# Expert weights split in three pieces, placed by a table; four-tile loops on ScalarE and VectorE; x in four slots

## The chip, the core and the metric

The kernel runs on one core of a Trainium2 chip. Its engines are TensorE (matmuls; PE in the profile, with PEld for the loads of its stationary operand), VectorE (DVE), ScalarE (ACT), GpSimd (POOL) and SyncE (SP), and 16 DMA engines that SP, ACT and POOL hand transfers to. Each engine works through its own list of instructions in order, and they meet at semaphores alone. An engine's sequencer also does what the profile does not count as busy: register arithmetic, branches, loads of registers from memory, waits, and handing out DMAs. The metric is the device time of one execution in microseconds (us).

## The reference

Cut to what matters (B = 8 batches of 256 rows of 512; 2048 tokens for the second part; E = 32 experts, 8 for each token, inner width I = 192):

```python
x = x + xattn(layernorm(x), ctx)          # attention over 8 batches; not touched by the change
xt = layernorm(x).reshape(-1, 512)        # 2048 tokens
probs = softmax(xt @ gate_w.T)            # 32 experts
full_w = top-8 of probs, scaled to sum 1, zero elsewhere
g = silu(einsum('th,ehi->eti', xt, w_gate))
u = einsum('th,ehi->eti', xt, w_up)
y = einsum('eti,eih->eth', g * u, w_down)
out = x + einsum('eth,te->th', y, full_w)
```

## The kernel before

**Two stages.** The first runs over the 8 batches (attention, layer norm, router). GpSimd scatters each normalised row, with its 32 expert weights and its token number behind it (512 + 33 floats), into the DRAM tensor `x_sorted`, once for each of its 8 experts and ordered by expert. The second stage is the expert layer. It runs over tiles of 128 sorted rows: 144 tiles in this data, 4 to 6 for each of the experts. Small tables, made on VectorE at the end of the first stage, say for each tile where its rows begin (`x_row`), which expert it belongs to, and what is to be done beside it.

**Precision.** Each matmul operand is a float32 split in two: a high part rounded to float32r (`_hi`, written by ScalarE with a copy) and the rest (`_lo`, by a subtraction on VectorE). Each product is then three matmuls (hi*hi, hi*lo, lo*hi). This holds for the tile's rows (`xT_hi`, `xT_lo`), for the activations (`aA_hi`, `aA_lo`, `aB`) and for the weights of each expert: `w_raw` (loaded), `w_hi` and `w_lo`, each in two halves for experts of even and odd number, with 1536 columns of gate and up and 1024 of down.

**One tile j**, as `ffn` of each engine has it:

- SP, `load_tile`: one register load of the row number (L365); four DMAs of the 128 x 512 floats (L373) and one of the 33 floats behind each row (L375), into slot j % 8. It first waits until VectorE's product of tile j - 8 is done (`act_ready`).
- PE: the gate and up product of tile j (12 matmuls, L1228, L1229, L1232); the transposes of tile j - 1's activation (L1188, L1189); the down product of tile j - 2 (5 matmuls, L1205 to L1209). Ahead of the last, its sequencer waits for the `_lo` part of that activation and for the bank (L1199). Ahead of the first it loads two registers, the count of experts that are needed and the half of the weights (L1214).
- ACT: silu of tile j (L632), `xT_hi` of tile j + 2 (L611), the high part of the activation of j - 1 (L616, L617), evacuation of y of j - 2 (L624). Then, where the table says so, the load of coming raw weights (`load_coming_raw`, two DMAs, L301 and L303), the copy of an expert's down weights (L520) and of its gate and up weights (L525). L630 is its register load, of two values.
- DVE: the transposition of tile j + 2 in blocks of 32 (L961); a register load of three values (L979); where the table says so the subtraction for an expert's down weights (L745) and gate and up weights (L751); a copy of the token numbers out of the slot (L992); silu * up * weight (L995); `xT_lo` of j + 2 (L965); the low parts of the activation of j - 1 (L972, L973).
- POOL: an indirect DMA that adds y of tile j to the rows of `out` that the token numbers name (L465). At an expert's first tile it waits until all earlier adds have landed.

**Where the weights are split.** At the first tile of expert e the tables name expert e + 1. ACT copies its gate and up columns at the end of that tile's step and its down columns in the next, and issues the raw load of expert e + 3 in the step after. DVE follows one step behind each: one piece of 1536 columns and, a step later, one of 1024.

**What sets the order.** All is written by hand. `run_tiles` unrolls 8 tiles, and then loops over eights with two conditional bodies of 4 tiles, as many as the data needs (36 fours here, out of at most 40); all five engines use it.

## Time and profile before

| | us |
|---|---|
| median of 3 runs | 860.26 |
| lowest and highest | 858.43, 863.49 |
| the profiled execution, as timed | 863.78 |
| its span, first to last instruction | 862.1 |
| PE busy in the span | 731.4 |
| DVE, ACT, POOL busy | 578.6, 436.5, 369.0 |

The span is 1.7 us shorter than the time of the same execution. The first stage takes about the first 265 us, and the tiles run from there to the end, at a granted TensorE clock of 1.00 of full speed for nearly all of it. In the lists, a start is in us from the start of the span; a second number is a duration; an entry in brackets is the idle time of that engine ahead of the instruction, and what ended it. "issue" means that nothing which the profile shows was waited for, which leaves the engine's own sequencer. A line name that ends in q (SPq, DVEq, ACTq, PEldq) is work of such a sequencer.

### The profile page before, as it was taken

The page shows a single profiled execution, that of the slowest core. Times are in us where ns is not written, and L with a number is a line of the kernel's source. Part 1 is how long each engine was busy: PE and PEld are TensorE (multiplying, and loading weights), DVE is VectorE, ACT ScalarE, POOL GpSimd, SP SyncE. Part 2 cuts the span into 40 slices and gives each one's busy share as a digit, 9 for nine tenths or more (in the row PEclk, how much of TensorE's full clock was granted, in tenths as well). Part 3 has the DMA queues.
Part 4 walks back from the last instruction along what each step waited for, and adds up shares of the span by engine and source line. Part 5 has one row for each costly group of instructions (what it writes and reads, how often), then busy time and mean ns, then how long its engine had stood idle before and what let it go on. Part 6 is the DMA issues. An engine that isn't in the chain of part 4 may idle for free.

```text
span 862.1 us, 21273 instructions
## 1 busy us (share of the span) xinstructions
PE 731.4 (85%) x3655; PEld 590.7 (69%) x3656; DVE 578.6 (67%) x1464; ACT 436.5 (51%) x1021; POOL 369.0 (43%) x294
## 2 busy tenths in 40 slices
PE   7998788795554389999999999999999989989994
PEld 5554444454344378888788788888878878878883
DVE  5584665575434266777877767877787777777773
ACT  2771544254110155566655565656655665655652
POOL 1015644765447233434344443434434443443443
PEclk9998999996776699999999999999999999999998
DMA  9976644554466479999999999999999999999975
GB/s 303 369 229 253 228 160 175 228 177 181 168 227 214 144 129 211 247 217 212 208 243 200 209 224 202 197 202 251 206 212 236 226 193 227 231 205 199 198 123 73
DMA packets 174394, 179.73 MB, mean 208 GB/s; under 512 B 36864, under 2 KB 128768, under 8 KB 174368
## 3 DMA queue, kind: packets, MB, share of 16 engines
q0 software_dynamic: 30976, 73.48, 39.2%
q1 hardware_dynamic: 119248, 68.09, 30.7%
q10 hardware_dynamic: 24144, 37.89, 14.0%
q8 instruction: 8, 0.13, 0.1%
q14 instruction: 18, 0.15, 0.0%
HBM read 92.25 MB, written 87.13 MB: 208 GB/s over the span
## 4 chain that ended last, share of the span: by engine, by line
PE 62%; issue 12%; DVE 7%; another core or an unknown queue 5%; SPq 4%; ACT 3%; DVEq 2%; DMA 2%; ACTq 1%; POOL 1%; POOLq 0%
PE bank L1228 12%; PE bank L1229 10%; PE bank L1232 10%; PE bank L1205 4%; PE bank L1206 3%; PE bank L1207 3%; PE bank L1209 3%; PE bank L1208 3%; SPq L373 2%; PE bank L1060 2%; PE bank L1188 2%; PE bank L1189 2%; PE bank L1126 1%; PE bank L1132 1%
## 5 line engine op out<-in xcount | busy, mean ns | idle before, releaser
L465 POOL DMA_INDIRECT out_dram<-ctx_all,tile_token x144 | 233.2, 1619 | 336.7 <-ACT ctx_all L624 182.2
L1228 PE MATMUL bank<-w_hi,xT_hi 128*128 x576 | 202.5, 351 | 39.6 <-issue 26.3
L1229 PE MATMUL bank<-w_lo,xT_hi 128*128 x576 | 196.6, 341 | 0.0
L420 POOL DMA_INDIRECT x_sorted<-xn_kept,slots x112 | 116.8, 1043 | 135.8 <-issue 87.1
L1228 PEld LDWEIGHTS bank<-w_hi,xT_hi 128*128 128x128 f32 x576 | 109.6, 190 | 69.4 <-issue 66.1
L632 ACT ACTIVATE probT<-bank 128x192 f32<-128x192 f32 x144 | 47.1, 327 | 164.2 <-PE bank L1232 127.1
L1232 PE MATMUL bank<-w_hi,xT_lo 128*128 x576 | 124.5, 337 | 0.0
L961 DVE STREAM_TRANSPOSE x_all<-x_all 128x512 f32<-128x512 f32 x146 | 103.9, 711 | 30.0 <-DMA x_all<-x_sorted 20.4
L611 ACT ACTIVATE xT_hi<-x_all 128x512 fp32r<-128x512 f32 x146 | 91.5, 627 | 62.9 <-DVE x_all L961 61.6
L1229 PEld LDWEIGHTS bank<-w_lo,xT_hi 128*128 128x128 f32 x576 | 109.9, 191 | 2.8
L1232 PEld LDWEIGHTS bank<-w_hi,xT_lo 128*128 128x128 f32 x576 | 103.1, 190 | 0.0
L965 DVE TENSOR_TENSOR xT_lo<-x_all,xT_hi 128x512 fp32r<-128x512 f32 x146 | 100.6, 689 | 1.7 <-issue 0.7
L995 DVE SCALAR_TENSOR_TENSOR probT<-probT,x_all,bank 128x192 f32<-128x192 f32 x144 | 59.0, 410 | 56.8 <-ACT probT L632 51.7
L624 ACT ACTIVATE ctx_all<-bank 128x512 f32<-128x512 f32 x144 | 85.7, 595 | 19.3 <-PE bank L1209 14.5
L751 DVE TENSOR_TENSOR w_lo<-w_raw,w_hi (+1 forms) x32 | 56.2, 1758 | 40.1 <-issue 39.0
L1205 PE MATMUL bank<-w_hi,aA_hi 128*128 x144 | 69.1, 480 | 15.1 <-issue 8.8
L1206 PE MATMUL bank<-w_lo,aA_hi 128*128 x144 | 56.8, 395 | 0.0
L1207 PE MATMUL bank<-w_lo,aB 128*128 x144 | 56.6, 393 | 0.0
L1209 PE MATMUL bank<-w_hi,aB 128*128 x144 | 56.3, 391 | 0.0
L1208 PE MATMUL bank<-w_hi,aA_lo 128*128 x144 | 56.2, 390 | 0.0
L525 ACT ACTIVATE w_hi<-w_raw (+1 forms) x32 | 47.6, 1488 | 12.5 <-issue 7.0
L1188 PE MATMUL bank<-ident,probT 128*128 128x128 f32 x144 | 39.4, 274 | 4.1 <-DVE probT L995 2.9
(198 smaller groups left out, 1123.2 us busy)
## 6 DMA issues: line engine op xcount, KB each, us to landing
x_all<-x_sorted SPq DMA_DIRECT2D x584, 64.0 KB
w_raw<-in_w_gate_up_dram ACTq DMA_DIRECT2D x28, 768.0 KB
w_raw<-in_w_down_dram ACTq DMA_DIRECT2D x28, 512.0 KB
x_sorted<-pad_rows SPq DMA_DIRECT2D x1, 8720.0 KB, 31.3
x_all<-in_x_dram SPq DMA_DIRECT2D x8, 512.0 KB
ctx_all<-in_ctx_dram SPq DMA_DIRECT2D x8, 512.0 KB
out_dram<-x_all SPq DMA_DIRECT2D x8, 512.0 KB
w_raw<-in_w_gate_up_dram SPq DMA_DIRECT2D x4, 768.0 KB
```

The lines of the kernel that those rows point to most:

```text
L420: pool.indirect_dma_start(out=x_sorted, out_offset=bass.IndirectOffsetOnAxis(ap=to[:, u, k:k + 1], axis=0), in_=rows[:, u, :], in_offset=N ...
L465: pool.indirect_dma_start(out=out, out_offset=bass.IndirectOffsetOnAxis(ap=tile_token[:, k:k + 1], axis=0), in_=y_sb[:, i, :], in_offset=N ...
L611: act_e.activation(xT_hi[:, s, :], xb[:, s, :], ACT.Copy).then_inc(S["xT_hi_ready"], 1)
L624: act_e.activation(y_sb[:, i, :], bank[6 + i % 2][:], ACT.Copy).then_inc(S["y_evac"], 1)
L961: dve.transpose(xb[:, i % 2, :].rearrange("p (c b t) -> p b c t", c=HC, b=HC), xg[:, i, :]).then_inc(S["xT_ready"], 1)
L965: dve.tensor_tensor(xT_lo[:, s, :], xb[:, s, :], xT_hi[:, s, :].bitcast(F32), ALU.subtract).then_inc(S["xT_lo_ready"], 1)
L1205: pe.matmul(out_y, aA_hi[:, s, :], part(w_hi, GU_END, DA_END), start=True, stop=False)
L1206: pe.matmul(out_y, aA_hi[:, s, :], part(w_lo, GU_END, DA_END), start=False, stop=False)
L1207: pe.matmul(out_y, aB[:, s, :], part(w_lo, DA_END, WCOLS), start=False, stop=False)
L1228: pe.matmul(out_gu, xT_hi[:, s, c * P:(c + 1) * P], gate_up(w_hi, c), start=(c == 0), stop=False)
L1229: pe.matmul(out_gu, xT_hi[:, s, c * P:(c + 1) * P], gate_up(w_lo, c), start=False, stop=False)
L1232: m = pe.matmul(out_gu, xT_lo[:, s, c * P:(c + 1) * P], gate_up(w_hi, c), start=False, stop=(c == HC - 1))
```

## The change

It touches the second stage and the tables ahead of it.

- **Pieces.** `w_raw`, `w_hi` and `w_lo` become six buffers: `gu_raw`, `gu_hi`, `gu_lo` with four pieces of 768 columns (gate and up of two experts in two pieces each), and `down_raw`, `down_hi`, `down_lo` with two of 1024.
- **Table.** For each tile one number tells VectorE how many gate and up pieces and how many down pieces are to be done by then, and the expert. Within an expert, the due count rises by one gate and up piece at its second tile, by another at its third, and by one down piece at its fourth, all of the next expert. With four tiles or more for each expert there is one piece a tile, in three tiles one after another. ScalarE's number is that of the tile after, and has a bit for the expert's first tile. Each engine keeps counts of what it has done in registers, and compares.
- **Register loads.** One value a tile on DVE (was three), ACT (two) and PE (two); the parts are taken out of the number with shifts and masks. PE works out half and count from one number.
- **Raw load.** ACT issues it at the first tile of an expert, for the expert after the next.
- **Token numbers.** The copy L992 and its wait are gone; POOL's add takes them from the slot itself.
- **x.** The 512 floats of a tile go to one of four slots, and SP waits for the transposition of tile j - 4. The 33 floats behind them keep eight slots, are issued two tiles later than the rows, and wait until the add of tile j - 8 has landed, and for the load of j - 4. So SP has two more waits a tile, each of which raises a counter (`wait_apart`).
- **Loops.** ACT and DVE unroll 8 tiles and then loop over fours (`run_quarters`); PE, SP and POOL stay with eights.

```diff
-        xg = x_all[:, 0:SLOTS, :]
+        xg = x_all[:, 0:4, :]
...
+        def run_quarters(eng, step):
+            turns = load_turns(eng)
+            for k in range(SLOTS):
+                step(k // 4, k % 4)
+            with eng.Fori(2, NT // 4) as q:
+                with eng.If(q < turns):
+                    for k in range(4):
+                        step(q, k)
...
+            def load_x(eight, k):
+                i = k % 4
+                sp.reg_load(row_reg[i], x_row[0:1, bass.ds(SLOTS * eight + k, 1)])
...
-                    sp.wait_ge(S["act_ready"], SLOTS * (eight + n - 1) + i + 1)
+                if not is_before(eight, k, 4):
+                    sp.wait_ge(S["xT_ready"], SLOTS * eight + k - 3)
...
-                sp.dma_start(xw[:, i, :], rows[:, H:RW]).then_inc(xg_loaded[i], 16)
+            def load_w(eight, k):
+                if not is_before(eight, k, SLOTS):
+                    wait_apart(sp, "sp_passed", (added[k % 4], 16 * (quarter(eight, k) - 1)))
+                if not is_before(eight, k, 4):
+                    wait_apart(sp, "sp_passed", (xw_loaded[k % 4], 16 * quarter(eight, k)))
+                sp.dma_start(xw[:, k, :], rows_at(k)[:, H:RW]).then_inc(xw_loaded[k % 4], 16)
...
-                    for k in range(2, 6):
-                        load_tile(eight, k)
+                    for k in range(4):
+                        load_w(eight, k)
+                        load_x(eight, k + W_BEHIND)
...
             def ffn(q, k):     # ACT, after evac_y
+                split_gu_hi(read_bits(act_e, gu_due_reg, due_reg, 7, 0, 2 * E))
+                split_down_hi(read_bits(act_e, down_due_reg, due_reg, 1, 63, E))
+                load_coming_raw(read_bits(act_e, first_reg, due_reg, 0, 1, 1))
...
+            def load_coming_raw(is_first):
+                with act_e.If(is_first > 0):
+                    e = act_e.snap(coming_reg, min_val=4, max_val=E - 1)
+                    wait_apart(act_e, "act_passed", (S["gu_ready"], 2 * e - 2), (S["down_ready"], e - 1), (S["raw_loaded"], 32 * e))
+                    load_raw(act_e, e, act_e.snap(e & 1, min_val=0, max_val=1))
...
+            def split_gu_lo(gu_due, level=0):     # DVE; ACT's split_gu_hi has the same form
+                done = dve.snap(gu_done_reg, min_val=4, max_val=2 * E)
+                with dve.If(done < gu_due):
+                    wait_apart(dve, "dve_passed", (S["gu_hi_ready"], done + 1))
+                    piece = dve.snap(done & 3, min_val=0, max_val=3)
+                    dve.tensor_tensor(gu_lo[:, bass.ds(piece, 1), :], gu_raw[:, bass.ds(piece, 1), :],
+                                      gu_hi[:, bass.ds(piece, 1), :].bitcast(F32), ALU.subtract).then_inc(S["gu_ready"], 1)
+                    dve.reg_alu(gu_done_reg, gu_done_reg, 1, ALU.add)
+                    if not level:
+                        split_gu_lo(gu_due, 1)
...
-                pe.reg_load([found_reg, half_reg[i]], tile_needs[0:1, bass.ds(j, 1), :].rearrange("p a b -> p (a b)"))
+                pe.reg_load(found_reg, experts_in[0:1, bass.ds(j, 1)])
                 pe.reg_alu(experts_reg[i], found_reg, 1, ALU.max)
+                pe.reg_alu(half_reg[i], experts_reg[i], 1, ALU.add)
+                pe.reg_alu(half_reg[i], half_reg[i], 1, ALU.bitwise_and)
+                pe.reg_alu(gu_need_reg, experts_reg[i], 2, ALU.mult)
```

```order
L979 TENSOR_LOAD dve_needs
L980 ISA
L984 COMPARE_AND_BRANCH
L236 REGISTER_ALU
L745 ISA [waits down_hi]
L745 TENSOR_TENSOR w_lo<-w_raw,w_hi 128x1024
L984 UNCONDITIONAL_BRANCH
L293 ISA
L987 COMPARE_AND_BRANCH
L236 REGISTER_ALU
L751 ISA [waits gate_up_hi]
L751 TENSOR_TENSOR w_lo<-w_raw,w_hi 128x1536
```

And after:

```order
L1045 TENSOR_LOAD dve_due
L308 REGISTER_ALU
L310 REGISTER_ALU
L311 ISA
L1017 COMPARE_AND_BRANCH
L237 REGISTER_ALU
L1020 REGISTER_ALU [waits gu_hi_ready]
L1020 ISA
L1020 TENSOR_TENSOR gu_lo<-gu_raw,gu_hi 128x768
L1022 ISA
L1017 COMPARE_AND_BRANCH
L237 REGISTER_ALU
```

The one subtraction of 1536 columns stood last, behind the place of the down piece; now a piece of 768 stands first, a second comparison stands nested behind it, and the down piece (still 1024 columns) follows after that.

**The order on SP** in the tile loop, from the small DMA of the 33 floats to the first large one of the next rows; before:

```order
L375 ISA
L375 DMA x_all<-x_sorted 128x33
L365 ISA
L365 TENSOR_LOAD x_row
L366 ISA
L373 ISA [waits act_ready]
L373 DMA x_all<-x_sorted 32x4x128
```

And after:

```order
L378 ISA [waits added1,xw_loaded1]
L399 DMA x_all<-x_sorted 128x33
L383 ISA
L383 TENSOR_LOAD x_row
L378 ISA [waits xT_ready]
L390 DMA x_all<-x_sorted 32x4x128
```

The small DMA, which waited for nothing, has two waits ahead of it and belongs to the tile two before the rows that follow; the rows wait for the transposition where they waited for the product.

## Rows read from the trace of the kernel before

**Rows 1.** Two stretches: busy PE, PEld, DVE, ACT, POOL; clock, DMA share, GB/s.

```profile
318.00:453.00 135.00, 126.77 (x656) 110.88 (x655) 101.50 (x226) 78.24 (x188) 55.23 (x35) 0.99 1.00 220
500.00:800.00 300.00, 281.50 (x1476) 246.88 (x1475) 228.28 (x500) 178.72 (x422) 124.86 (x77) 1.00 0.99 214
```

**Rows 2.** PE: first transpose of two tiles; then its count, first and last start.

```profile
496.92 0.27 PE L1188 MATMUL bank<-ident,probT 128*128 128x128 f32 x1
...
500.39 0.27 PE L1188 MATMUL bank<-ident,probT 128*128 128x128 f32 x1
...
L1188 PE MATMUL bank<-ident,probT x78: 272/272/272, 500.4 to 798.5; 128*128 128x128 f32 x78
```

**Rows 3.** Groups of instructions, 300 to 800 us: count, busy us, mean ns.

```profile
L751 DVE TENSOR_TENSOR w_lo<-w_raw,w_hi x28 | 49.2, 1758 | 36.9 <-issue 35.8 <-ACT w_hi L525 1.1
...
L525 ACT ACTIVATE w_hi<-w_raw x28 | 41.7, 1489 | 11.7 <-issue 6.6 <-DMA w_raw<-in_w_down_dram 5.0
...
L745 DVE TENSOR_TENSOR w_lo<-w_raw,w_hi x28 | 33.1, 1183 | 0.0
...
L992 DVE COPY tile_token<-x_all 128x1 int32<-128x1 int32 x129 | 18.5, 144 | 24.5 <-issue 21.8 <-DMA out_dram<-ctx_all,tile_token 1.8
```

**Rows 4.** DVE in order of time, ahead of one gate and up subtraction.

```profile
494.94 0.71 DVE L961 STREAM_TRANSPOSE x_all<-x_all 128x512 f32<-128x512 f32 x1
497.05 1.76 DVE L751 TENSOR_TENSOR w_lo<-w_raw,w_hi  x1 [1.40 <-issue]
```

**Rows 5.** ACT in order of time, around one load of raw weights.

```profile
503.05 0.43 ACTq L301 DMA_DIRECT2D w_raw<-in_w_gate_up_dram  x1
...
505.31 0.33 ACT L632 ACTIVATE probT<-bank 128x192 f32<-128x192 f32 x1 [2.60 <-PE bank L1232]
```

**Rows 6.** Register loads: ns min/median/max, first and last start.

```profile
L979 DVEq TENSOR_LOAD <-dve_needs x144: 741/1076/1679, 294.6 to 844.7; - x144
...
L1214 PEldq TENSOR_LOAD <-tile_needs x144: 532/540/1479, 265.7 to 842.5; - x144
...
L365 SPq TENSOR_LOAD <-x_row x146: 4/276/1049, 264.2 to 826.7; - x146
```

**Rows 7.** SP's small DMA in 318:453 and 500:800: count, first and last.

```profile
L375 SPq DMA_DIRECT2D x_all<-x_sorted x38: 68/364/569, 320.0 to 451.8; - x38
...
L375 SPq DMA_DIRECT2D x_all<-x_sorted x78: 14/364/737, 501.4 to 799.7; - x78
```

**Rows 8.** SP's waits in these two stretches: total us, times, longest.

```profile
SPq L373 <- DVE probT L995: 1.7, 1, 1.7
...
SPq L373 <- DVE probT L995: 32.3, 31, 2.4
```

**Rows 9.** SP in order of time: tiles 2, 7, 10, 11 and 145.

```profile
290.69 1.86 SPq L373 DMA_DIRECT2D x_all<-x_sorted  x4
...
305.47 3.59 SPq L373 DMA_DIRECT2D x_all<-x_sorted  x4
...
318.06 1.78 SPq L373 DMA_DIRECT2D x_all<-x_sorted  x4
...
321.06 1.86 SPq L373 DMA_DIRECT2D x_all<-x_sorted  x4
...
827.91 1.88 SPq L373 DMA_DIRECT2D x_all<-x_sorted  x4
```

**Rows 10.** DVE in order of time: transposition of tiles 2, 7 and 145.

```profile
294.60 0.71 DVE L961 STREAM_TRANSPOSE x_all<-x_all 128x512 f32<-128x512 f32 x1 [2.32 <-DMA x_all<-x_sorted]
...
312.81 0.71 DVE L961 STREAM_TRANSPOSE x_all<-x_all 128x512 f32<-128x512 f32 x1 [2.37 <-DMA x_all<-x_sorted]
...
845.29 0.71 DVE L961 STREAM_TRANSPOSE x_all<-x_all 128x512 f32<-128x512 f32 x1
```

**Rows 11.** POOL in order of time: two adds, the second of a first tile.

```profile
500.09 1.55 POOL L465 DMA_INDIRECT out_dram<-ctx_all,tile_token  x1 [2.90 <-ACT ctx_all L624]
506.16 1.55 POOL L465 DMA_INDIRECT out_dram<-ctx_all,tile_token  x1 [4.51 <-issue]
```

306 lines of the change are left out of this document (157 added, 149 removed).

## The prediction

> **What bounds the kernel now.** I read first how long a tile takes, then who is late when it takes longer, then who could not go faster. The first stage is not touched; the tiles fill the span from about 265 us on. In 500 to 800 us PE is busy 281.5 of 300 us and DVE 228.3 [rows 1], but PE's busy time is modelled, so I take the distance between equal instructions. An undisturbed tile takes 500.39 - 496.92 = 3.47 us; 78 of them start between 500.4 and 798.5, so the mean is 298.1 / 77 = 3.87 us [rows 2]. So 0.40 us a tile is lost. There are 28 subtractions of each kind for 129 tiles [rows 3], one for 4.6 tiles, which makes the loss 1.8 us for each expert.
>
> Where it comes from: the long piece. After the transposition at 494.94 (ended 495.65) DVE stands idle for 1.40 us for its own sequencer and then subtracts for 1.76 us [rows 4]; the product for that tile (L995) and the low parts that PE's down product waits for are behind it on DVE. The 1.40 us are mostly the register load of three values, 0.74 to 1.68 us, behind the dispatch of the transposition, and two branches [rows 6]. PE then pays twice, as its own load of two values (0.54, at most 1.48 us) stands behind its wait ahead of the down product, and has to be done before the next tile's first matmul [rows 6]. ACT has one more: the sequencer hands out the raw weights from 503.05 on, 0.43 us for the first of two DMAs, and the next silu starts at 505.31 [rows 5].
>
> Who could not go much faster: **SP**. In 318 to 453 us it issues 38 small DMAs from 320.0 to 451.8, (451.8 - 320.0) / 37 = 3.56 us a tile [rows 7], and waits for only 1.7 us in all of it [rows 8]. So 3.52 us a tile is SP's own pace. In 500 to 800 us it needs (799.7 - 501.4) / 77 = 3.87 us, of which 32.3 us are waits: own pace (298.3 - 32.3) / 77 = 3.45. An undisturbed tile takes SP 321.06 - 318.06 = 3.00 us [rows 9]; the rest are hand-outs that stick, as the 3.59 us for four that otherwise take 1.86 [rows 9]. SP's own 3.48 us (mean of the two) is PE's 3.47. Today SP is ahead only because PE loses 0.40 us a tile.
>
> **The change, part by part.**
>
> *Pieces.* A piece of 768 columns is half of L751's and L525's 1536: 1758 / 2 = 0.88 us on DVE, 1489 / 2 = 0.75 on ACT [rows 3], both perhaps 0.03 more for the fixed part. The work stays the same in sum, but one tile now gets 0.88, 0.88 and 1.18 us in three tiles, instead of 1.76 and 1.18 in two. DVE's busy time a tile is 228.3 / 77.5 = 2.95 us with its share of the subtractions, (1.76 + 1.18) / 4.6 = 0.64 [rows 1, 3], so 2.31 without them and 2.17 without the copy of 0.14 (L992). With 0.88 that is 3.05, with 1.18 it is 3.35: both fit into 3.47 if the engine doesn't wait for its sequencer, while 2.31 + 1.76 = 4.07 did not. This takes the largest part of the 1.8 us an expert from PE.
>
> *Register loads.* One value takes SP 0.28 us, two take PE 0.54, three take DVE 0.74 at least and 1.08 in the median [rows 6]: some 0.25 us a value. I take 0.3 to 0.5 us off on DVE, 0.25 on ACT and PE; against it DVE gets some eight register steps and one comparison more, ACT about the same, PE three. At 0.08 us a step (below) that gives 0.3 to 0.6 us back, in the sequencer, beside the engine's work except ahead of a piece. I count nothing for the sum of both (bounds: 0.3 us a tile either way on the chain silu, product, low parts). The Trainium skill ("DMA: Bandwidth & Descriptors", latency and other measured facts) gives a register load from memory a floor of about 600 ns, whatever its size; by that rule one value would save DVE 0.14 us at least time and PE nothing, and SP's median of 0.28 us speaks against it.
>
> *Raw load.* It stays on ACT, at 1.1 us of its sequencer for each expert, now in the tile that also has a piece of 0.75 us where it had none. That keeps part of the loss: 0.3 to 1.0 us an expert, 0.07 to 0.22 a tile. It is issued one expert (at least 4 tiles, 13.9 us) ahead of its use. 1.31 MB take 6.1 us at the whole 214 GB/s of that stretch and 12.2 at half of it [rows 1], so it arrives in time.
>
> *x in four slots.* The rows can be fetched four tiles ahead, 13.9 us. From SP's first hand-out to the transposition it took 294.60 - 290.69 = 3.9 us at tile 2 and 312.81 - 305.47 = 7.3 us at tile 7, where DVE waited for the data both times [rows 9, 10]. Both fit into 13.9; cost nothing, unless SP itself is late.
>
> *Two more waits on SP.* They are the one thing that the change adds to the engine with no reserve. The order shows the same steps else. SP's 3.00 us are 1.86 for four DMAs, 0.36 for the small one, 0.28 for the register load, and 0.50 for some six register steps [rows 6, 7, 9]: 0.08 each. Two waits that raise a counter, each with its register step at times, then cost 0.16 to 0.26 us; I take 0.18. What is queued behind them are the rows of tile j + 2, and DVE waits for those. Whether the waits themselves hold: the add of tile j - 8 has to land; an add lands within 506.16 - 500.09 = 6.1 us of its issue even when the next one waits for it [rows 11], and SP is a lot later than that.
>
> *Rest.* The tables need about as many small steps as before, while SP is fetching the first tile. Two more empty rounds of the loop on ACT at the end: 0.4 us by my estimate.
>
> **The sum.** SP's new pace is 3.48 + 0.18 = 3.66 us. Nothing ahead of tile 10 is faster for SP, whose rows it hands out at 318.06 [rows 9]. 135 tiles later it reaches tile 145: 318.1 + 135 x 3.66 = 812.2 us, where it was at 827.9 with a lead that it now doesn't have. From hand-out to transposition 5 us (bounds 3.9 and 7.3), to the end as before 862.1 - 845.3 = 16.8 us [rows 10], and 0.4: 812.2 + 5 + 16.8 + 0.4 = 834.4 us of span. That is 27.7 less than 862.1. The profiled execution took 863.78 us, so it would be 836.1; the median of the runs is 860.26, so it would be **832.6**. PE's own sum agrees: floor 3.47 and 0.07 to 0.22 for the raw load are 3.54 to 3.69 us a tile.
>
> **The rivals.**
>
> *PE sets the pace* (821). SP's sticking hand-outs become rarer, as its fetches no longer run 17 us ahead (827.91 to 845.29 today [rows 9, 10]), or its waits cost next to nothing. Then a tile takes 3.47 us and some 0.1 for what is left on ACT, 3.58. Tiles 7 to 145 took 845.29 - 312.81 = 532.5 us [rows 10], 3.86 each; 138 x 3.58 = 494 is 38.5 less: 822. With nothing left at all it is 138 x 3.47 = 479, 807. For it: 32.3 us of waits show that SP has gone at PE's pace. Against it: in 318 to 453 us SP never waits and is no faster than 3.52.
>
> *Half a gain* (846). The pieces still start late: after a transposition come a load, six register steps, a branch, and only then 0.88 us. If DVE loses 0.5 us at each of three pieces, and ACT the raw load's 1.0, 2.5 us of 4.6 x 3.47 = 16.0 hardly fit, and with the SP waits added in the same tiles 3.75 to 3.77 us a tile remain: 138 x 0.1 = 13.8 less, 846.
>
> *The DMA engines set the pace* (no change, 857 to 861). Their busy share is 0.99 at 3.87 us a tile [rows 1]. If that were a wall, no tile could be shorter, and SP's sticking hand-outs would be its sign. The Trainium skill (its first page, "Trainium Kernel Development and Optimization", key constraints) says that the queues of SP, ACT and POOL run on the same 16 engines and interleave; by this rule three queues add up and the share is a sum over queues. Against it as a wall: the share is 1.00 in the first stretch too [rows 1], where SP fetched a tile in 3.56 us for 135 us.
>
> *Slower than before: the ring of eight and four slots.* A tile's add has to land before the 33 floats of the tile eight later are fetched, and the rows of the tile ten later stand behind that on SP. Around this ring: evacuation to add at most 4.5 us (an expert's first tile), landing 6.1 [rows 11], SP 0.5, fetch 7.3 [rows 9, 10], and about 4.5 tiles from transposition to evacuation, 15.6 at 3.47. That is 34.0 us for ten tiles, 3.4 a tile, each at its worst. It decides from 34.7 us on and makes the kernel slower from 10 x 3.87 = 38.7, that is if waits and landings together take 4.7 us longer than the worst read here, at every tile. At 7 us longer it is 4.10 us a tile: 138 x 0.24 = 33 more, 893.
>
> **How the numbers follow.** SP's pace 0.42; PE's pace 0.21; half a gain 0.18; DMA wall 0.12; the ring 0.07. The prediction is that of the first, 832.6, and its own range 822 (own pace 3.45 and 0.13 more) to 845 (3.52 and 0.26, fetch 7.3). The range of 8 in 10 takes in the second from 813 on, and the third; it ends where the wall begins, at 856. What a measurement can tell from no change is about 0.5%, 4.3 us. Faster by more than that: 0.42 + 0.21 + 0.18 and a sliver of the wall's case, 0.82. Within it: 0.10. Slower: 0.08.
>
> **What the profile after would show.** Right: SP's small DMA once in 3.6 to 3.7 us with almost no waits; DVE waits for x at many transpositions, as at tiles 2 and 7; two pieces of about 0.9 and one of 1.2 us in three tiles; PE's undisturbed tile still 3.47. Wrong: SP waits for `xT_ready` in long sums (then PE or DVE sets the pace); SP's wait for the adds shows up (the ring); DMA share 0.99 at an unchanged 3.86 (the wall); idle time for "issue" ahead of each piece of over 0.5 us (half a gain); ACT waits for raw weights, which I priced at nothing.

## The result, and the profile after

Four executions of the changed kernel beside four of the kernel before on the same chip: median 900.85 us (894.5 to 911.39) against 861.88 (858.43 to 875.75), a ratio of 1.044 with a 95% interval of 1.033 to 1.056. The ratio is of the fast executions alone: 911.39 and 875.75, each over 1.5% above the fastest of its kernel, are left out of it. The prediction was 832.6 us and faster; the kernel became slower. The profiled execution took 911.39 us, of which the span is 909.4, the longest of the four; so where sizes matter I use a second trace of the same kernel, from the experiments (829.9 us of span, on another chip; the kernel before has 790.7 on one like it). Both tell the same story.

The tile loop first, as PE's first transposition of each tile: count, duration and the first and last start, of the changed kernel, then of the kernel before on the same chip, then of the kernel before on a chip of the experiments.

```profile
L1248 PE MATMUL bank<-ident,probT x144: 270/272/476, 300.6 to 893.9; 128*128 128x128 f32 x144
```
```profile
L1188 PE MATMUL bank<-ident,probT x144: 272/272/331, 296.5 to 849.1; 128*128 128x128 f32 x144
...
L1188 PE MATMUL bank<-ident,probT x144: 272/272/415, 225.2 to 777.7; 128*128 128x128 f32 x144
```

143 tiles apart, (893.9 - 300.6) / 143 = 4.15 us a tile after, (849.1 - 296.5) / 143 = 3.86 before, and 3.86 again on the other chip. I call this the mean tile from here on; it can be read from one row of any trace. 593.3 - 552.6 = 40.7 us of the 47.3 us by which the span grew are in it. Now the two stretches of [rows 1] again (busy PE, PEld, DVE, ACT, POOL; clock, DMA share, GB/s):

```profile
318.00:453.00 135.00, 120.34 (x619) 102.80 (x618) 92.88 (x186) 75.42 (x183) 50.74 (x33) 1.00 0.90 192
500.00:800.00 300.00, 273.38 (x1357) 236.20 (x1357) 203.31 (x402) 167.80 (x402) 111.28 (x71) 0.95 0.91 198
```

PE fell from 281.5 busy us to 273.4 of 300 and DVE from 228.3 to 203.3; the DMA engines' share, which was 0.99 to 1.00, is 0.90 and 0.91. Nobody is busier. So somebody waits more, and the page says who: two lines of its costliest groups (count, busy us, mean ns, idle before and its releasers), and the chain of the work that ended last.

```profile
L1004 DVE STREAM_TRANSPOSE x_all<-x_all 128x512 f32<-128x512 f32 x146 | 103.9, 712 | 76.3 <-DMA x_all<-x_sorted 70.0
...
L656 ACT ACTIVATE xT_hi<-x_all 128x512 fp32r<-128x512 f32 x146 | 91.6, 628 | 101.2 <-DVE x_all L1004 79.0
...
PE 25%; DMA 23%; issue 16%; SPq 9%; DVE 7%; another core or an unknown queue 7%; ACTq 4%; ACT 3%; DVEq 3%; POOL 2%; POOLq 1%
DMA out_dram<-ctx_all,x_all 12%; DMA x_all<-x_sorted 10%; SPq L390 6%; PE bank L1290 3%; PE bank L1291 3%; PE bank L1294 3%; PE bank L1265 2%; POOL x_sorted L448 1%; PE bank L1143 1%; PE bank L1151 1%; SPq L399 1%; PE bank L1185 1%; PE bank L1269 1%; SPq L383 1%
```

The transposition of x now waits 70.0 us for rows (20.4 before), and ScalarE, which takes its high parts, 79.0 us for the transposition (61.6 before). The chain was 62% PE before; now it is 25% PE and 23% DMA, with the adds at the head of its lines and the rows behind them. That is the pattern of the rival that I had given 0.07. SP's waits for the adds, 500 to 800 us, then its small DMA in the same stretch (answering [rows 7, 8]):

```profile
SPq L238 <- DMA out_dram<-ctx_all,x_all: 40.6, 22, 3.2
...
L399 SPq DMA_DIRECT2D x_all<-x_sorted x70: 7/364/705, 501.8 to 798.1; - x70
```

Where did time go within one turn of the ring? Tiles 51 and 61, all engines in order of time: transposition of tile 51, evacuation of its result, its add, the small DMA of tile 59 (which waited for that add), the rows of tile 61 behind it, and their transposition.

```profile
498.38 0.71 DVE L1004 STREAM_TRANSPOSE x_all<-x_all 128x512 f32<-128x512 f32 x1
...
515.81 0.60 ACT L669 ACTIVATE ctx_all<-bank 128x512 f32<-128x512 f32 x1
...
523.25 1.55 POOL L493 DMA_INDIRECT out_dram<-ctx_all,x_all  x1 [7.40 <-issue]
...
528.82 0.36 SPq L399 DMA_DIRECT2D x_all<-x_sorted  x1
529.78 1.89 SPq L390 DMA_DIRECT2D x_all<-x_sorted  x4
...
540.12 0.71 DVE L1004 STREAM_TRANSPOSE x_all<-x_all 128x512 f32<-128x512 f32 x1 [3.31 <-DMA x_all<-x_sorted]
```

From 498.38 to 540.12 are 41.7 us for ten tiles, where undisturbed ones take 34.7. The add waited 523.25 - 516.41 = 6.8 us on GpSimd, because it is the first of an expert and the ones ahead of it had not landed; it landed and let SP go 5.6 us later; the rows took 540.12 - 529.78 = 10.3 us, for 3.31 of which DVE stood waiting.

One more thing grows out of the waits. In 500 to 800 us the granted TensorE clock is 0.95 of full speed, where it was 1.00. In the traces it is either at full speed or at half (2.4 or 1.2 GHz). In the second trace it is at half for 20.5 us of the tile loop, and in the same loop without the ring (run e1 below) never. Ahead of one such stretch, at 692.5 us, PE was busy only 5.33 of 10 us. At half speed PE does half the work, so up to 10 us of what the ring costs there come by way of the clock, an estimate from these stretches.

### The profile page after: what moved, and what is told of

Read it like the earlier page. It is cut to its first block, busy times and chain, and to the rows that moved or that the text cites. A ratio compares the mean times of both kernels' runs of the same rounds, so it can differ in the third digit from the quotient of the medians.

```text
span 909.4 us, 23919 instructions
## 1 busy us (share of the span) xinstructions
PE 761.1 (84%) x3655; PEld 604.0 (66%) x3656; DVE 567.6 (62%) x1351; ACT 442.0 (49%) x1051; POOL 363.7 (40%) x293
## 4 chain that ended last, share of the span: by engine, by line
PE 25%; DMA 23%; issue 16%; SPq 9%; DVE 7%; another core or an unknown queue 7%; ACTq 4%; ACT 3%; DVEq 3%; POOL 2%; POOLq 1%
DMA out_dram<-ctx_all,x_all 12%; DMA x_all<-x_sorted 10%; SPq L390 6%; PE bank L1290 3%; PE bank L1291 3%; PE bank L1294 3%; PE bank L1265 2%; POOL x_sorted L448 1%; PE bank L1143 1%; PE bank L1151 1%; SPq L399 1%; PE bank L1185 1%; PE bank L1269 1%; SPq L383 1%
## 5 line engine op out<-in xcount | busy, mean ns | idle before, releaser
L493 POOL DMA_INDIRECT out_dram<-ctx_all,x_all x144 | 227.4, 1579 | 385.2 <-ACT ctx_all L669 194.9
L1290 PE MATMUL bank<-gu_hi,xT_hi 128*128 x576 | 206.9, 359 | 21.2 <-issue 18.7
L1291 PE MATMUL bank<-gu_lo,xT_hi 128*128 x576 | 200.3, 348 | 0.0
L1290 PEld LDWEIGHTS bank<-gu_hi,xT_hi 128*128 128x128 f32 x576 | 113.0, 196 | 51.7 <-issue 47.7
L1294 PE MATMUL bank<-gu_hi,xT_lo 128*128 x576 | 125.2, 338 | 0.0
L1291 PEld LDWEIGHTS bank<-gu_lo,xT_hi 128*128 128x128 f32 x576 | 113.2, 197 | 2.9
L1294 PEld LDWEIGHTS bank<-gu_hi,xT_lo 128*128 128x128 f32 x576 | 104.4, 192 | 0.0
L669 ACT ACTIVATE ctx_all<-bank 128x512 f32<-128x512 f32 x144 | 85.6, 594 | 20.4 <-PE bank L1269 17.9
L1265 PE MATMUL bank<-down_hi,aA_hi 128*128 x144 | 70.8, 492 | 28.4 <-DVE aB L1039 17.2
L1248 PE MATMUL bank<-ident,probT 128*128 128x128 f32 x144 | 40.7, 282 | 30.0 <-DVE probT L1052 20.0
L1269 PE MATMUL bank<-down_hi,aB 128*128 x144 | 58.2, 404 | 0.0
L1267 PE MATMUL bank<-down_lo,aB 128*128 x144 | 58.0, 403 | 0.0
```

Of the source, the lines that this page charges most:

```text
L493: pool.indirect_dma_start(out=out, out_offset=bass.IndirectOffsetOnAxis(ap=xw[:, k, E:E + 1].bitcast(I32), axis=0), in_=y_sb[:, i, :], in_ ...
L669: act_e.activation(y_sb[:, i, :], bank[6 + i % 2][:], ACT.Copy).then_inc(S["y_evac"], 1)
L1265: pe.matmul(out_y, aA_hi[:, s, :], part(down_hi, 0, H), start=True, stop=False)
L1269: pe.matmul(out_y, aB[:, s, :], part(down_hi, H, DN), start=False, stop=True).then_inc(S["y_done"], 1)
L1290: pe.matmul(out_gu, xT_hi[:, s, c * P:(c + 1) * P], gate_up(gu_hi, c), start=(c == 0), stop=False)
L1291: pe.matmul(out_gu, xT_hi[:, s, c * P:(c + 1) * P], gate_up(gu_lo, c), start=False, stop=False)
```

## Experiments

The runs e1 to e4, e5 to e8 and e9 to e16 were made on three further chips, on which the kernel before takes nearly the same time: 793.9, 795.0, and 794.1 and 791.5 us in the median. On the last of them it was traced, with a mean tile of 3.86 as on the first. So I compare their times with each other; each ratio is to the kernel before beside it, and differences of medians across chips are good to some 3 us. The changed kernel runs at 829.5 there, its version with a token copy at 796.7. SP's totals of waits for adds below have one part that costs nothing: behind the last fetch SP waits once more for the last adds, 14 to 21 us in three or four waits in the kernels with the ring. Where I give a total "up to the last fetch", that part is taken off. The edits are shown in short form, cut to what matters. The expectations of the first four runs (e1 to e4) were written on the first chip's scale, where the kernel before takes 862; on these chips everything is some 67 us shorter, ahead of the tiles, and their times have to be read that much lower. Expectations speak of theories: 1 the ring; 2 four slots for x are too few; 3 pieces, branches and short loops cost; 4 the ring costs little on these chips; 5 to 9 are explained where they come up.

**e1_token_copy and e5_after_again: is it the ring?**

```diff
-  sp: wait added[k % 4] >= 16 * (quarter(eight, k) - 1)
+  sp: wait act_ready >= SLOTS * (eight - 1) + k + 1
+  dve: wait added[k] >= 16 * (q - 1)
+  dve.tensor_copy(tile_token[:, slot], token column of xw[slot])
-  pool: offsets from xw[:, k, E:E + 1]
+  pool: offsets from tile_token[:, k:k + 1]
```

> The changed kernel, but VectorE copies each tile's token numbers into a buffer of eight, as the kernel before does, and SP's fetch of the 33 floats waits for the product of tile j - 8 (act_ready) instead of its add; x stays in four slots, all else stays. Theory 1 (ring: SP's wait for the add of tile j - 8 holds back the rows of tile j + 2 behind it): the wait is gone, SP runs up to four tiles ahead, the time falls to what I had forecast for SP's own pace, 825 to 850 us. Theory 2 (four slots of x are too few for the fetch): no gain, 885 to 905. Theory 3 (the pieces, the nested branches or the four-tile loops cost the time on VectorE and ScalarE): no gain, 890 to 905.

> The changed kernel itself, unaltered, to stand beside the others on one chip. Theory 1 (ring): a tile takes 4.1 us here as well, and the time is 1.03 to 1.05 of the kernel before; the version with the token copy is below it by 25 to 45 us. Theory 4 (the table's pieces alone bring nothing, and the ring costs little on a chip with quicker transfers): within 1.5% of the kernel before.

Measured: 796.7 us, 1.005 of the kernel before (1.002 to 1.009), against 829.5, 1.043 (1.038 to 1.048) for the changed kernel. SP's and DVE's waits of the changed kernel, then DVE's in the token copy version:

```profile
SPq L238 <- DMA out_dram<-ctx_all,x_all: 97.9, 51, 9.3
...
DVE x_all L1004 <- DMA x_all<-x_sorted: 49.2, 29, 6.5
```

```profile
DVE x_all L1005 <- DMA x_all<-x_sorted: 14.5, 6, 5.2
```

The ring costs 33 us: with it gone DVE's waits for rows fall from 49.2 to 14.5 us. Up to the last fetch SP's waits for adds are 79.8 us of the 97.9, in 47 times. Theory 1 holds for the ring, 2 falls (x still has four slots), 4 falls. But 796.7 is not 832.6 / 860.3 of the kernel before, which would be 769: the pieces' gain of 28 us isn't there either. That was a second error, and the rest of the runs divide between the two. Theory 3, which foresaw no gain from this edit, is not the whole cause; these 28 us are what is left of it.

**e2_ahead_3 and e3_ahead_1: the ring's length.** `W_BEHIND = 2` becomes 3, and 1; the second has one more fetch behind the loop.

> The changed kernel with one number changed: SP issues the rows of tile j + 3, not j + 2, behind the 33 floats of tile j. Theory 1 (ring): the ring is eleven tiles long instead of ten; with the 41 us that it takes on average now, a tile takes 41 / 11 = 3.73 us instead of 4.1, some 50 us less: 845 to 865 us. Theory 2 (four slots): rows still at most four tiles ahead, and SP doesn't wait for slots now: little, 880 to 900. Theory 3 (pieces and loops): unchanged, 895 to 905.

> The changed kernel with the rows of tile j + 1 behind the 33 floats of tile j (and one more fetch behind the loop). Theory 1 (ring): nine tiles, 41 / 9 = 4.55 us a tile, some 60 us more: 945 to 975 us. Theories 2 and 3: slots and pieces are as they were, so at most 10 us more: 895 to 912.

Measured: 802.5 us (1.009, 1.005 to 1.013) and 879.1 (1.106, 1.099 to 1.113). A ring of 9, 10, 11 tiles gives 879, 830, 802: one tile less costs 50 us (60 expected), one more brings 27 (50 expected). The order is the ring's, the proportion isn't quite: a turn isn't of one length, it takes 9 x 4.43 = 39.9, 10 x 4.11 = 41.1 and 11 x 3.94 = 43.3 us by the mean tiles, since with more tiles in the ring it binds less often.

**e6_loading_alone: the other half of the change.** The kernel before with the changed loading and ring, splitting in its two long pieces.

> The kernel before with the loading of the changed kernel alone: x in four slots, the 33 floats fetched apart and eight tiles round, SP waiting for the add of tile j - 8, GpSimd reading the token numbers there, no copy on VectorE. The splitting stays in two long pieces. Theory 1 (ring): this part alone makes it slower, by the whole difference between the changed kernel and the version with the token copy: 1.03 to 1.05 of the kernel before, with SP waits for adds of 50 us and more. Theory 3 (pieces and loops cost the time): same as the kernel before, 0.99 to 1.01.

Measured: 800.9 us, 1.0075 (1.005 to 1.010). SP waits for adds 53.4 us, 35.8 of them up to the last fetch, yet it costs 6 us, not 33:

```profile
SPq L237 <- DMA out_dram<-ctx_all,x_all: 53.4, 25, 9.4
...
DVE x_all L976 <- DMA x_all<-x_sorted: 23.1, 15, 3.8
```

By its number this is theory 3's case, but e1 had spoken against it: there the pieces stayed and 33 us went with the ring. By theory 1's number it should have been 1.03 to 1.05. The ring needs a partner that is in the changed kernel and not here. Beside the pieces and the loops the two differ in when ScalarE issues an expert's raw weights, 1.31 MB: two tiles after an expert's first there, at the first here.

**e7_no_raw_loads, e16_token_copy_no_raw, e10_small_raw_loads: the raw weights.** Left out from the fifth expert on, with the waits for them, with the ring and without; then a sixteenth of their bytes in the same places.

```diff
-  load_coming_raw(...)                       # e7, e16; e10 keeps it
-  wait raw_loaded ahead of each high piece   # e7, e16
+  load_raw moves partitions 0:8 of 128       # e10
```

> The changed kernel without the loads of raw weights from the fifth expert on and without the waits for them (ScalarE and VectorE split what is there), 37 MB less through the DMA engines. Theory 1 (ring, whose landings are stretched by the bursts of 1.31 MB at each expert's first tile): adds land in 5 us and rows in 4 to 5 us at most tiles, SP's waits for adds fall to under 25 us in all, 30 to 50 us less than the changed kernel. If the hold of an expert's first add on GpSimd and the plain length of the ring do it alone: 5 to 15 us less, which is what ScalarE saves by not issuing them.

> The changed kernel with raw loads of the same number, place and waits, but of 8 of 128 partitions each (a sixteenth of the bytes, from the fifth expert on). It keeps what ScalarE's sequencer does and takes the burst away. Without either it was 756.4. If the burst is what costs (DMA): 756 to 775. If ScalarE's issuing costs: it keeps 28 times 1.1 to 2 us, 788 to 815.

> The version with the token copy (no ring) without the loads of raw weights from the fifth expert on and without the waits for them; with the ring the same was 756.4. Theory 8 (the ring costs only where a burst stretches the landings): no difference left, 748 to 760. If the ring costs its 33 us (829.5 - 796.7) whatever the landings: 720 to 730.

Measured: e7 756.4 us (0.954, 0.947 to 0.961), e16 760.9 (0.962, 0.957 to 0.968), e10 804.7 (1.013, 1.007 to 1.020). The tile row of e7:

```profile
L1245 PE MATMUL bank<-ident,probT x144: 271/272/415, 224.3 to 736.6; 128*128 128x128 f32 x144
```

(736.6 - 224.3) / 143 = 3.58 us a tile. Leaving the loads out saves 73 us, more than the 30 to 50 of theory 1. Three things follow. First, with no bursts the ring costs nothing (756.4 with it, 760.9 without it but with VectorE's copy; theory 8, within 1 us of its range). Second, both the bytes and their issue cost. By e10 the bytes cost 829.5 - 804.7 = 25 us and what ScalarE does to issue them 804.7 - 756.4 = 48, which is 1.7 us for each of 28. That division is rough: e10's small loads make ScalarE's next silu later than the whole ones do, by 14 us in all (worked out as below), so the issue costs less than 48 and the bytes more than 25. Without the ring, issue and bytes together cost 796.7 - 760.9 = 36 us, or 1.3 for each of 28. Third, SP's wait is not its price. In e10:

```profile
SPq L238 <- DMA out_dram<-ctx_all,x_all: 77.3, 30, 10.6
...
DVE x_all L1008 <- DMA x_all<-x_sorted: 8.1, 6, 2.1
...
ACT probT L681 <- DMA down_raw<-in_w_down_dram: 85.9, 28, 3.6
```

SP waits for the adds 77.3 us (56.6 up to the last fetch), and DVE for rows only 8.1: rows that start late still land in time here, where the weights are small. And ScalarE stands idle ahead of silu with the issue of weights as the last thing it did, 28 times, 85.9 us in all; the profile names their landing as what ended this, but silu waits for nothing of theirs.

**e8_raw_load_earlier, e9_ring_raw_earlier, e11_token_copy_best, e12_ahead_3_raw_earlier: ScalarE's side.** In the token copy version the engine looks like this around a load (issue, silu), with PE's last products of the tile ahead:

```profile
514.66 0.85 ACT L633 ACTIVATE gu_hi<-gu_raw  x1
516.28 0.40 ACTq L316 DMA_DIRECT2D gu_raw<-in_w_gate_up_dram  x1
516.88 0.39 ACTq L318 DMA_DIRECT2D down_raw<-in_w_down_dram  x1
519.00 0.33 ACT L678 ACTIVATE probT<-bank 128x192 f32<-128x192 f32 x1 [3.49 <-issue]
...
515.34 0.86 PE L1298 MATMUL bank<-gu_hi,xT_lo 128*128 x4
```

The products end at 516.20, silu starts at 519.00, 2.8 us late: a piece, two branches, two DMA issues, the loop's branch and the register load stand in a row ahead of it. I worked this lateness out for tiles 10 to 139, start of silu less end of the last product less the usual 0.04 us, and summed it over the tiles where it is more than 0.3 us: 29 us in the kernel before (e13), 85 in the changed one (e5), 88 in e1, 106 in e10, 1 in e7. The edit of e8 and e9 moves the issue one tile earlier, where ScalarE has no piece; e11 also puts the register load behind silu; e12 is e9 with `W_BEHIND = 3`.

```diff
-  act_due[:, 0:NTX - 1] = 2 * gu_due[:, 1:NTX] + is_first[:, 0:NTX - 1]
+  act_due[:, 0:NTX - 1] = 2 * gu_due[:, 1:NTX] + is_first[:, 1:NTX]
-  read_due(j); wait gu_done; silu          # e11 alone
+  wait gu_done; silu; read_due(j)
```

> The version with the token copy (first of the experiments), with ScalarE's issue of the raw weights one tile earlier: at the tile ahead of an expert's first, where ScalarE has no piece, instead of at the first, where it has one. Theory 5 (the pieces bring nothing because ScalarE's silu is late: a piece, two DMA issues, the loop's branch and the register load stand ahead of it, 2 to 2.8 us at such tiles, 88 us in all against 24 in the kernel before): the lateness falls by about 1 us an expert, 15 to 25 us less than 796.7 in that session, so 0.97 to 0.985 of the kernel before. Rival (DMA engines at 0.94 to 0.98 are the wall, whatever the engines do): unchanged, 1.00 to 1.01 of the kernel before.

> The changed kernel (ring kept) with the raw weights issued one tile earlier, nothing else. Theory 6 (the raw load in the tile of the first piece is the cause twice over: it makes silu late on ScalarE, and its burst of 1.31 MB falls together with the held add and the rows that the ring has kept back): 785 to 808 us, 20 to 40 us less than the changed kernel's 829.5. If only ScalarE's lateness moves, as between the two versions with the token copy (796.7 to 778.8): 18 us less, 808 to 815. If the ring alone decides: 825 to 832.

> The version with the token copy and the raw load one tile earlier (778.8), and ScalarE loads its register of the table behind the silu, not ahead of it. Theory 5: silu late 45.9 us in that version, a good part of it a register load of 0.3 to 1 us after the loop's branch; moved behind silu it runs beside it: 5 to 12 us less, 766 to 775. Rival: the load comes ahead of the piece anyway, which then starts later: unchanged, 776 to 782.

> The changed kernel with rows three tiles behind the 33 floats (the ring of eleven) and the raw load one tile earlier; no token copy on VectorE. Theories 1 and 6: the ring of eleven tiles with short landings no longer binds, VectorE has 0.14 us a tile less than in the version with the copy: 765 to 785 us. If the wait for the adds still holds the rows back at each expert: 785 to 800.

Measured: e8 778.8 us (0.980, 0.975 to 0.985), e9 813.3 (1.024, 1.016 to 1.031), e11 775.5 (0.979, 0.972 to 0.985), e12 787.7 (0.989, 0.981 to 0.997). In e8 the same place:

```profile
509.44 0.42 ACTq L318 DMA_DIRECT2D down_raw<-in_w_down_dram  x1
510.84 0.33 ACT L678 ACTIVATE probT<-bank 128x192 f32<-128x192 f32 x1 [3.02 <-issue]
...
508.34 0.86 PE L1298 MATMUL bank<-gu_hi,xT_lo 128*128 x4
```

Silu is 510.84 - 509.20 = 1.6 us late instead of 2.8, 46 us in all, and the kernel 18 us faster. Theory 5 holds, and so the DMA share isn't a wall: it is 0.97 in e1 and in e8 alike, from 300 to 700 us, at mean tiles of 3.88 and 3.75 (theory 6's second half fails: e9 gained 16 us, what ScalarE's side gives, and the ring kept its 34 us, 813.3 - 778.8). The register load brought 3 us where I looked for 5 to 12, and 3 us between two chips can't be told from nothing, though the lateness fell to 25 us. e12 came out at the end where the adds still hold the rows back. e11 is faster than both kernels, by 2.1% than the one before; it relies on experts of four tiles or more, since a shorter one could make ScalarE wait for a piece that VectorE reaches only behind it.

**e4_split_alone: a trap on the way.** The pieces with the whole loading of the kernel before; VectorE's loop had to go back to eight tiles for its eight slots.

> The split into three pieces by the table alone, with the loading of the kernel before: x and the 33 floats in eight slots, one wait for the product of tile j - 8, token numbers copied by VectorE, VectorE's loop over eight tiles (ScalarE's over four). Theory 1 (ring): no ring, the gain of the pieces is seen: SP's own pace without the two waits, 3.48 us a tile, or PE's 3.58: 815 to 840 us, at or some us below the version with four slots. Theory 2 (four slots): the same, 815 to 840, and well below the version with four slots and the token copy. Theory 3 (pieces and loops): slower than the kernel before, 875 to 905.

Measured: 879.7 us, 1.101 (1.090 to 1.112), slower than any theory had it, and 83 us above e1. The pieces alone can't be that, since e1 has them too. What DVE waited for ahead of its transpositions, one such place, and the page's instruction queue, then that queue in e1:

```profile
  issue: 66.1, 16
...
501.09 0.71 DVE L985 STREAM_TRANSPOSE x_all<-x_all 128x512 f32<-128x512 f32 x1 [5.56 <-issue]
...
q14 instruction: 111, 0.91, 0.3%
```

```profile
q14 instruction: 20, 0.16, 0.1%
```

Once in a round of eight tiles DVE stands still for nothing that the profile names, 4.1 us in the mean, 66.1 in all, and once 20.6 us behind the loop; and the instruction queue brings 111 packets instead of 20. I take it that the loop of eight with nested branches no longer fits where the engine keeps its code and is fetched anew in each round, which no run shows directly; the changed kernel, with its loops of four, has 19 packets. The granted clock falls with it, to 0.95 over the tile loop where e1 has 1.00. So e4 says nothing of the split, and a version with four-tile loops and eight slots of x wasn't tried.

**e14_gpsimd_issues_raw and e15_token_copy_gpsimd_raw: another engine issues the weights.**

```diff
-  act: load_coming_raw(is_first)
+  pool, ahead of the add of tile j, if an expert begins at j + 2:
+      wait gu_ready, down_ready, raw_pool; load_raw(pool, e, ...)
```

> The changed kernel (ring kept, 829.5) with the raw weights of the third expert on issued by GpSimd, ahead of the add two tiles before an expert's first, instead of by ScalarE; the bursts stay whole. Theory 7 (of the 73 us that the raw loads cost, 829.5 - 756.4, ScalarE's issuing makes 48 and the burst, with the ring, 25): silu late by under 20 us, and 785 to 805 us. If the bytes cost the time, whoever issues them: 815 to 830. If GpSimd's issues hold up the adds behind them: SP's waits for adds grow over 98 us, above 830.

> The version with the token copy, the register load behind silu, and GpSimd issuing the raw weights as in the run ahead. Theory 7: neither ring nor issuing on ScalarE is left, only the pieces' own time and the bursts: 3.6 to 3.7 us a tile, 755 to 768. Rival (the DMA engines at 0.95 to 1.0 bound what is left): 770 to 780, no better than the version with the load one tile earlier (775.5).

Measured: e14 853.8 us (1.076, 1.068 to 1.084), e15 834.6 (1.054, 1.048 to 1.060): theory 7's times were missed, the last rival of e14 was right (silu's lateness did go, to 23 us), and e15 was missed by theory and rival alike. GpSimd in e14, two issues and the adds around them:

```profile
469.14 1.10 POOL L316 DMA_DIRECT2D gu_raw<-in_w_gate_up_dram  x1
469.95 1.06 POOL L318 DMA_DIRECT2D down_raw<-in_w_down_dram  x1
472.05 1.72 POOL L508 DMA_INDIRECT out_dram<-ctx_all,x_all  x1 [1.04 <-issue]
474.07 2.08 POOL L508 DMA_INDIRECT out_dram<-ctx_all,x_all  x1 [0.30 <-issue]
483.83 1.56 POOL L508 DMA_INDIRECT out_dram<-ctx_all,x_all  x1 [7.68 <-DMA out_dram<-ctx_all,x_all]
```

The add at 483.83 stood 7.68 us for the two ahead of it, issued at 472.05 and 474.07 right behind 1.31 MB on the same queue. Over tiles 10 to 137 an add now starts 4.4 us behind its evacuation in the mean (2.8 in e5), and in e15 8.9 (3.5 in e1). In e15 nothing on SP waits for adds, but ScalarE does, since it writes results into four slots that the adds empty:

```profile
ACT ctx_all L686 <- DMA out_dram<-ctx_all,tile_token: 116.9, 70, 5.8
```
The page "DMA: Bandwidth & Descriptors" of the Trainium skill (queues, rings and completion order) says that each DMA engine takes turns between the queue rows, while it takes the descriptors of one ring in order; by that rule weights on ScalarE's queue share the way with the adds, and on GpSimd's they stand ahead of them. These traces agree, as far as the waits above tell.

**e17_ring_raw_later and e18_token_copy_raw_later: the burst's place.** On a fifth chip (kernel before 876.3 us). The issue two tiles later, as in the kernel before, with the ring and without:

> The changed kernel (ring kept) with the raw weights issued two tiles later, at an expert's third tile, as in the kernel before; everything else as changed. The difference to the run that follows is the ring's price with the burst in this place; at the first tile it was 33 us (829.5 against 796.7), one tile earlier 34 (813.3 against 778.8), in the kernel before with its long pieces 6. Theory 9 (the burst's place decides: from an expert's third tile on it comes behind the adds on which the held one waits): a difference of 5 to 15 us. Rival (the short pieces decide, wherever the burst is): 28 to 38 us.

> The version with the token copy (no ring) with the raw weights issued two tiles later. By themselves the weights now have two tiles and some, 7 to 9 us, until ScalarE's first piece of them in an expert of four tiles, and land in 8 to 12: ScalarE waits for them in places, 0 to 25 us more than the 796.7 of the load at the first tile: 797 to 822.

Measured: 882.1 us, 1.003 (0.999 to 1.007), and 876.9, 1.001 (0.998 to 1.004). The ring's price is 5 us, give or take 4, as in e6, instead of 33 (the mean tiles of the two traces, 3.92 and 3.84, would give 11, but e17's trace is of its longest execution); the changed kernel with nothing but this is level with the kernel before. Theory 9 holds, with one gap: the changed kernel itself was not run on this chip, so 5 and 33 are from different chips. (On the first chip, whose first stage is slow too, it lost 4.4%.) ScalarE now waits for the weights themselves, which is likely why it isn't better:

```profile
ACT gu_hi L632 <- DMA down_raw<-in_w_down_dram: 30.4, 13, 3.3
```

The landings fit. Worked out over tiles 10 to 137 from the evacuations, the adds and their packets, one add in ten lands later than 8.1 us in e5 and 8.2 in e9, where the ring costs 33 and 34 us, and than 6.4 in e17 and 6.4 in e6, where it costs 5 and 6. The longest hold of an add ahead of its start doesn't divide them so: 7.6 us in e5, but 5.0 in e9 and in e17, and 4.0 in e6. This points at the landings and not at the hold.

**e13_before_again:** the kernel before, for its trace.

> The kernel before, unaltered, for a trace of it on the chip of the experiments. All theories: 788 to 799 us, a tile of 3.83 to 3.87 us between tiles 10 and 143, as in the trace on the first chip; silu late by 20 to 30 us in all. If the tile is shorter here, part of what I read as the loading's small cost alone is the chip's.

Measured: 792.4 us, mean tile 3.86 as on the first chip; its DVE waits 12.8 us for rows. So the 3.91 of e6 stands against 3.86, and its small price is unlikely to be an accident of its chip.

## Why the prediction was wrong, point by point

Two steps of the sum failed. The first is the wait for the add of tile j - 8, put at nothing because "SP is a lot later than that": SP waited 58.7 us for adds up to the last fetch, and the ring that this closes cost 33 us (e5 against e1), in company with the raw weights, whose bytes were at nothing too. The second is the gain of the pieces, 27.7 us in the sum, which never came (e1: 796.7 where it would be 769), because the raw load on ScalarE costs more than its "0.3 to 1.0 us an expert".

**What bounds the kernel now.** PE's undisturbed tile of 3.47 us was right and stands after. SP's own pace was put at 3.66. In e7, with SP's new order unchanged, SP waits 1.1 us in all over tiles 12 to 142 and takes 3.56 us a tile, so 3.66 was 0.1 too much. Whether SP or PE sets the 3.58 us of that run stays open, since neither waits for the other to speak of; in e8 and e11 SP waits 14 and 10 us for free slots, so there it isn't the bound. In the changed kernel SP's pace in 500 to 800 us, (798.1 - 501.8) / 69 - 40.6 / 69 = 3.71, looks like my 3.66, but it is not what the tiles take: they take 4.15, with the waits. The reading of the 3.00 us tile was wrong as well. "The rest are hand-outs that stick" holds for little of it: over tiles 12 to 142 of the kernel before, four hand-outs take 0.09 us more than 1.86 in the mean, and a register load 0.12 more than 0.28. The sticking ones do go with the bursts: four hand-outs took over 2.2 us 18 times in e5 and once in e7.

**Pieces.** The sizes were near: 0.94 us against 0.88, 1.23 against 1.18.

```profile
L1020 DVE TENSOR_TENSOR gu_lo<-gu_raw,gu_hi x52 | 48.8, 938 | 10.4 <-issue 7.2 <-ACT gu_hi L632 2.9
...
L1032 DVE TENSOR_TENSOR down_lo<-down_raw,down_hi x25 | 30.6, 1226 | 16.2 <-issue 12.3 <-ACT down_hi L643 3.9
```

The gain was not there, because I costed the pieces on VectorE and left ScalarE with one clause. The failed term is the raw load, "0.3 to 1.0 us an expert": measured 1.7 with the ring (e10, at most) and 1.3 without it, bytes included (e1, e16), and 0.6 of it (18 us over 28 experts, e8) only because it shares a tile with a piece. My own rival "half a gain" had the raw load in it, at 1.0, and the pace 3.75 that e8 gives. That the pace agrees is in part luck: it put 1.5 us an expert on VectorE's starts and 1.0 on ScalarE, while in e1 VectorE waits only 8.4 us over 28 experts for its own sequencer ahead of its pieces, 0.3 each.

**Register loads.** VectorE's one value takes 0.307 us in the median instead of 1.08 for three:

```profile
L1045 DVEq TENSOR_LOAD <-dve_due x144: 300/307/1011, 298.5 to 889.3; - x144
```

That is half of the 600 ns which the Trainium skill ("DMA: Bandwidth & Descriptors", latency and other measured facts) gives as a floor; the trace decides. I had counted nothing for the sum. What lay in where ScalarE's load stands is 3 us by e11, within the noise.

**The bytes of the raw weights.** "It arrives in time", costed at nothing: the weights did, within 7.4 to 12.6 us of at least 13.9, but the adds and rows beside them did not. This is the step that turned the sign: with the burst back in an expert's third tile the changed kernel is level with the kernel before (e17). I asked who reads a transfer and not who shares the 16 engines with it, though the change moves the burst from an expert's third tile to a first one: some 25 us by e10, and a ring that costs 33 us where it costs 5 with the burst in its old place.

**x in four slots** at nothing: right. SP doesn't wait for a slot of x in the changed kernel; without the ring it does, 28.3 us, and DVE waits for rows 14.5 us where it did 12.8 before.

**Two more waits on SP.** As instructions 0.28 us instead of 0.18: the small DMA of an undisturbed tile comes 3.28 us behind the last one where it was 3.00. Both lines are of SP's order of time:

```profile
539.58 0.36 SPq L399 DMA_DIRECT2D x_all<-x_sorted  x1
...
542.86 0.36 SPq L399 DMA_DIRECT2D x_all<-x_sorted  x1
```

That they hold nothing up, "SP is a lot later than that", was false: 73.0 us of waits, 58.7 of them up to the last fetch, and 33 us of time in e5 against e1.

**The ring, at 0.07.** Mechanism, place and the point from which it makes the kernel slower (38.7 us for ten tiles) were right. The terms, as foreseen and in the turn shown above: transposition to evacuation 15.6 and 18.0; evacuation to add 4.5 and 6.8; landing 6.1 with SP's 0.5, and 5.6 with 1.0; fetch 7.3 and 10.3. In sum 34.0 and 41.7. I called the first "each at its worst". But the longest landing of an add in that trace, from its packets, is 6.8 us, and in the changed kernel 9.1. And 15.6 was an undisturbed 4.5 tiles, where the same trace, worked out over tiles 10 to 143, has 18.5 us or 4.8 tiles in the mean and never less than 16.3. It also doesn't need to happen "at every tile": two bursts fall into each turn.

**The DMA wall, half a gain.** The share of 0.99 was no wall: it fell to 0.91 in a slower kernel and e11 has 0.98 with 3.74 us a tile. What I listed as signs was of use: SP's waits for adds, and DVE's idle time, named the ring at first sight.

## What to carry to other kernels

When a wait for a buffer is put onto a queue that works in order, lay out the whole turn from fetch to release, take each landing as it is beside the heaviest transfer that can fall together with it, and compare that with the number of tiles between. Cost a burst to everybody on the DMA engines, and when a change moves it by a tile or two, ask which landings it now meets: here its place decided between 5 and 33 us, on different chips. A wait in a list costs only what arrives too late behind it, so read the engine that uses the data; and look at what a sequencer has to do in a row (branches, register load, DMA issues) ahead of the short instruction that all others wait for.

## What the runs showed of the hardware

One program, and 862 us on the first chip, 792 to 795 on three others, 876 on a fifth. Between the first chip and one of the three all of the difference lies ahead of the tiles. The first 250 us of the kernel before on either (columns as in [rows 1]):

```profile
0.00:250.00 250.00, 192.83 (x864) 118.72 (x865) 145.80 (x476) 102.94 (x232) 114.51 (x128) 0.90 0.64 227
```

```profile
0.00:250.00 250.00, 217.63 (x1055) 145.70 (x1057) 179.07 (x584) 121.86 (x274) 141.79 (x155) 0.95 0.81 274
```

The granted clock is 0.90 and 0.95 of the 2.4 GHz level, the traffic 227 and 274 GB/s, and the tiles begin at 296.5 and 225.2 us; from there on both take 552.6 and 552.5 us for 143. What makes the first stage slower on a chip I didn't find.

In e4 VectorE's loop of eight tiles with nested branches stood still for 66.1 us in 16 times without a single long instruction. It shows only as idle time for "issue" at the loop's start and as 111 packets of the instruction queue instead of 20; that the code outgrew its place is my reading.

The TensorE clock fell where TensorE had to wait: 0.95 over the tile loop of e4 and 0.98 over that of e5, against 1.00 in e1, with 2,700 matmuls in each. They took 544.9, 533.8 and 520.9 us of PE's busy time.
